# Message stage of a graph network kernel: units of four tiles and one of a single tile in place of four and three

## The chip, the cores and the metric

The kernel runs on one core of a Trainium2 chip. The time is that of one execution in microseconds of device time (us); a lower one is better. Its engines are PE (TensorE, matrix products), DVE (VectorE), ACT (ScalarE), POOL (GpSimd) and SP (SyncE, which here only issues DMAs). Each works through its own instructions in order and waits for others by semaphores.

## The reference

Two graph layers on 6250 nodes with 128 features, over 200000 edges sorted by destination:

```
h = relu(layernorm(x));  x = x + gcn2(relu(gcn1(h)))          # layer 0
h = relu(layernorm(x))                                         # layer 1
msg = relu(concat(h[src], edge_attr) @ W1 + b1)                # edge_attr: 32 columns
agg = segment_sum(msg, dst) / max(count, 1)
x = x + relu(concat(h, agg) @ W2 + b2)
```

The change touches only the third line and the sum in the fourth, the message stage. `h @ W1[:128] + b1` is made once per node, so a message is `relu(that[src] + edge_attr @ W1[128:])`.

## The kernel before, in words

The message stage treats the edges in two ways at once. The first half of the edges is sorted, earlier in the kernel, into 24 ranges; inside a range they lie in 49 tiles (blocks) of 128, each with edges whose sources fall in one block of 128 nodes. The other half is gathered: chunks of 512 edges, whose source rows POOL fetches by four indirect DMAs a chunk (`gather_messages`, line 779).

A loop runs over twelve pairs of ranges; eleven are one loop body, and the last is written out for itself. `UNIT_TILES = [4, 3] * 7` (line 84) cuts a range's 49 tiles into 14 units, so a pair has 28 units and 30 steps. In step u each engine has, in this order:

- PE: for an even chunk, the attribute products of two later chunks (`products_of`, line 1159); the transpose of unit u's attributes (`turn_attr`, 1183); a chunk's sums (`sums_of`, 1168); `block_products` of unit u-1, which is one product of the attributes with the weights, up to 512 columns (1190), and one product a tile of a one-hot matrix of sources with the node rows (1194); `block_sums` of unit u-2, one product a tile of a one-hot matrix of targets with the messages (1206).
- ACT: `message` of a chunk (1458), `stage_attr` of unit u+1 (1464), `take_attr` of unit u (1471), `block_message` of unit u-1 (1478), and at some steps the lows: `store_lows` (1300, 1302) and `load_lows` (1453).
- DVE: `source` of unit u, the one-hot matrix of sources (2187); `rest_of` unit u-2 (2177); a chunk's one-hot matrix; `target` of unit u-1 (2192); `add` (2157) and `products_in` (2200) of a chunk.

Pairs have 16 chunks, the last 24; `chunk_of(u, chunks)` spreads them evenly over the steps.

The "lows" are the numbers 0 to 127 of each edge's source in its block. They are turned by PE (`turn_lows`, at steps 7 and DU + 10), written to memory by ACT one step later, and read back spread over all partitions in four parts of `LO_UNITS = 4` units each. Parts 0 and 1 of the second range are loaded at step DU - 4, part 2 at DU - 2, part 3 at DU; those of the next pair's first range at steps 2 DU - 1, 2 DU and 2 DU + 1, the last three of a pair. `load_lows` first waits on ACT until the store has landed, and for parts 2 and 3 until part 0 or 1 of the same range has landed (they share a semaphore). `source` of a part's first unit waits for the part.

SP reads the next pair's two blocks of sorted edges (`load_blocks`, 617), each 833 KB, and the chunks' attributes (621), when semaphores of DVE and ACT let it.

Of the kernel before, what the change touches and what calls it, by code (L numbers as in the profile page):

```python
# [25 lines left out]
TC = 4  # L26
CE = TC * P
SLOTS = 8
# [34 lines left out]
SB = (N + P - 1) // P  # L63

RANGES = 24
RT = 32
DT = RANGES * RT
# [13 lines left out]
LATE_STEPS = (1, 2, 6, 8)  # L81
VISIT_ROWS_AT = 8
OWN_EDGE = 8192.0
UNIT_TILES = [4, 3] * 7
DU = len(UNIT_TILES)
LO_UNITS = 4
LO_PARTS = -(-DU // LO_UNITS)
LO_BLOCKS = sum(UNIT_TILES[:LO_UNITS])
LO_TURNED_AT = (7, DU + 10)
# [6 lines left out]
LAST_CHUNKS = (TURNS - FIRST_TURN) * SLOTS - (PAIRS - 1) * PAIR_CHUNKS  # L96
# [35 lines left out]
assert NP >= SB * P - 1 + P and TARGETS < SB * P and EP >= E and NCH % SLOTS == 0 and NT % (2 * HT) == 0  # L132
assert STRIPS % 2 == 1 and LAST_WIDTH % W == 0 and len(VISITS) == NW and KEYS <= 512 and SB == 12 * SEGS + 1 and STRIP % P == 0
assert SEG % BANKS == 0
assert DT % (SLOTS * TC) == 0 and LAST_CHUNKS % SLOTS == 0 and RANGES % 2 == 0 and DU % 2 == 0 and sum(UNIT_TILES) == SB and RT % 2 == 0
assert DT * P >= RANGE_ROWS
assert RANGES % 2 == 0 and LO_BLOCKS * P * 2 <= RT * ROW_WORDS * 4
assert all((b - a) * RT <= 512 for a, b in BLOCK_GROUPS) and RT * P < OWN_EDGE and RANKS_BEFORE_STARTS % RANK_BATCH == 0
# [4 lines left out]
def build(nc, t, out):  # L143
    with ExitStack() as ctx:
# [67 lines left out]
        def carve(columns, dt=F32):  # L212
            a = used[0]
            used[0] += columns
            assert used[0] <= SB * STRIP
            return region_a[:, a:a + columns].bitcast(dt)
# [21 lines left out]
        block_lo = [carve((SB + 1) // 2, BF16) for _ in range(2)]  # L238
        unit_attr = [carve(max(UNIT_TILES) * DE) for _ in range(2)]
        message_rows = carve(NT - DT, I32)  # L240
# [261 lines left out]
        def unit_tiles(u):  # L502

            first = sum(UNIT_TILES[:u])
            return first, UNIT_TILES[u]

# [1816 lines left out]
```

How the kernel before makes its waits and increments, by code:

```python
        def tables_stored(engine, n):  # L489
            for q in range(2):
                engine.wait_ge(tab_stored[q], 16 * ((NG + 1 - q) // 2) * (n + 1))
# [21 lines left out]
        def mixed_of(engine):  # L514
            engine.wait_ge(edges_read, 1)
            return engine.value_load(mixed_i[0:1, 0:1], min_val=0, max_val=1)
# [27 lines left out]
        def widen(engine, k, p):  # L545
            a, b = pieces_of(k)[p]
            at = k * len(PIECES) + p
            second = len(half_pieces(k))
            if p in (0, 1) and k:
                engine.wait_ge(C["loaded_a"], k * 16)
            if p in (second, second + 1) and k:
                engine.wait_ge(C["loaded_b"], k * 16)
            if at >= WIDE_SLOTS:
                engine.wait_ge(consumed, at - WIDE_SLOTS + 1)
            if len(APPLIED[k]) == 2:
                to, of = wide[:, at % WIDE_SLOTS, 0:b - a], count_pair[:, :, a:b].rearrange("p s h d -> p h s d")
            else:
                to, of = wide[:, at % WIDE_SLOTS].rearrange("p h s d -> p (h s) d")[:, 0:b - a], counts[0][:, a:b]
            if WIDENED_BY[p] == "act":
                nc.scalar.activation(to, of, ACT.Copy).then_inc(widened["act"], 1)
            else:
                nc.vector.tensor_copy(to, of).then_inc(widened["dve"], 1)
# [1 line left out]
        @block.sync  # L565
# [16 lines left out]
            load_bias("L0_gnn_b1")  # L582
            sp.wait_ge(rows_reduced, 1)
            sp.dma_start(tiles_dram[0].rearrange("(p q) -> p q", p=CR), row_min[0:CR, :]).then_inc(tiles_moved, 16)
```

## Time and profile before

| | us |
|---|---|
| three runs: median (lowest, highest) | 2529.35 (2528.84, 2536.39) |
| the profiled execution: its time | 2535.55 |
| its span, first to last instruction | 2533.6 |
| PE busy | 2189.9 (86%) |
| PE weight loads busy | 1792.7 (71%) |
| DVE busy | 1891.2 (75%) |
| POOL busy | 1840.9 (73%) |
| ACT busy | 1213.8 (48%) |
| mean granted clock of PE, full speed being 1 | 0.938 |

The busy times are of the profiled execution and overlap. "PE" are the matrix products, "PEld" the loads of their stationary operand. The granted clock has two levels, 2.4 and 1.2 GHz.

### The profile page before, as it was taken

The page shows a single profiled execution, that of the slowest core. Times are in us where ns is not written, and L with a number is a line of the kernel's source. Part 1 is how long each engine was busy: PE and PEld are TensorE (multiplying, and loading weights), DVE is VectorE, ACT ScalarE, POOL GpSimd, SP SyncE. Part 2 cuts the span into 40 slices and gives each one's busy share as a digit, 9 for nine tenths or more (in the row PEclk, how much of TensorE's full clock was granted, in tenths as well). Part 3 has the DMA queues.
Part 4 walks back from the last instruction along what each step waited for, and adds up shares of the span by engine and source line. Part 5 has one row for each costly group of instructions (what it writes and reads, how often), then busy time and mean ns, then how long its engine had stood idle before and what let it go on. Part 6 is the DMA issues. An engine that isn't in the chain of part 4 may idle for free.

```text
span 2533.6 us, 47549 instructions
## 1 busy us (share of the span) xinstructions
PE 2189.9 (86%) x15568; PEld 1792.7 (71%) x15569; DVE 1891.2 (75%) x3625; ACT 1213.8 (48%) x3289; POOL 1840.9 (73%) x1687
## 2 busy tenths in 40 slices
PE   0453799999999998699996699999999999999996
PEld 0132578997666898588885578778777877787785
DVE  6996999999888884644447577777777777777776
ACT  5842345665555775555553244444443444343340
POOL 0857777888888887777777577777777777777770
PEclk9665899999999999999997799999999999999998
DMA  9413223443332442488874243434343343434332
GB/s 366 155 42 128 72 73 123 156 149 123 121 119 109 145 173 74 133 311 307 318 275 158 85 142 103 124 118 127 117 121 118 96 126 116 138 98 122 116 90 61
DMA packets 127166, 357.85 MB, mean 141 GB/s; under 512 B 34082, under 2 KB 77831, under 8 KB 117687
## 3 DMA queue, kind: packets, MB, share of 16 engines
q10 hardware_dynamic: 24752, 186.56, 19.4%
q0 software_dynamic: 56880, 85.25, 13.0%
q1 hardware_dynamic: 45369, 84.00, 9.5%
q8 instruction: 83, 1.36, 0.2%
q14 instruction: 82, 0.67, 0.1%
HBM read 229.75 MB, written 125.93 MB: 140 GB/s over the span
## 4 chain that ended last, share of the span: by engine, by line
PE 67%; DVE 15%; DMA 6%; ACT 5%; issue 4%; POOL 2%; ACTq 0%; DVEq 0%; POOLq 0%; SPq 0%
PE ps_feat L1063 7%; PE ps_node L1063 6%; PE ps_sum L1168 6%; PE ps_node L1078 5%; PE ps_extra L1206 5%; DVE region_c L2002 4%; PE ps_feat L1078 4%; PE ps_node L1190 3%; PE pre_banks L1051 3%; PE ps_node L1194 3%; DMA rows_or_lows<-block_lows 3%; ACT rows L1282 3%; PE ps_feat L1190 3%; PE ps_sum L1194 3%; PE ps_sum L1190 3%
## 5 line engine op out<-in xcount | busy, mean ns | idle before, releaser
L797 POOL DMA_INDIRECT permuted<-rows_or_lows,slot_of_edge x768 | 923.4, 1202 | 234.1 <-issue 156.1
L779 POOL DMA_INDIRECT rows<-table,region_a x800 | 788.6, 986 | 291.1 <-issue 218.7
L2002 DVE TENSOR_TENSOR region_c<-iota_key,region_c 128x1568 bf16<-128x1568 f16 (+1 forms) x327 | 355.3, 1087 | 0.0
L1375 ACT ACTIVATE region_a<-pre_banks 128x392 bf16<-128x392 f32 x392 | 195.4, 501 | 198.8 <-PE pre_banks L1051 191.2
L1063 PE MATMUL ps_node<-region_a,region_b 128*128 128x256 bf16 (+1 forms) x1911 | 263.6, 268 | 0.0
L1063 PE MATMUL ps_feat<-region_a,region_b 128*128 128x256 bf16 x1764 | 254.4, 274 | 0.0
L563 DVE CAST wide_counts<-region_a 128x1024 fp32r<-128x1024 bf16 (+2 forms) x163 | 117.3, 724 | 156.7 <-PE ps_node L1078 65.7
L1206 PE MATMUL ps_extra<-msg_parts,target_hot 128*128 128x256 f32 x1176 | 222.4, 305 | 1.3 <-DVE msg_parts L2177 1.3
L561 ACT ACTIVATE wide_counts<-region_a 128x1024 fp32r<-128x1024 bf16 x150 | 158.4, 1060 | 121.3 <-PE ps_node L1078 52.7
L1168 PE MATMUL ps_sum<-onehot,rows 128*128 128x64 f32 x1600 | 209.2, 275 | 0.3 <-issue 0.2
L1168 PEld LDWEIGHTS ps_sum<-onehot,rows 128*128 128x128 f32 x1600 | 204.5, 199 | 5.5 <-issue 4.6
L2192 DVE TENSOR_TENSOR target_hot<-consts,region_a 128x512 fp32r<-128x512 f32 x336 | 207.3, 617 | 1.0
L1063 PEld LDWEIGHTS ps_node<-region_a,region_b 128*128 128x128 bf16 x1911 | 176.2, 97 | 28.7 <-issue 1.5
L1063 PEld LDWEIGHTS ps_feat<-region_a,region_b 128*128 128x128 bf16 x1764 | 169.5, 97 | 28.9 <-issue 0.4
L1478 ACT ACTIVATE msg_parts<-ps_node 128x512 fp32r<-128x512 f32 x120 | 65.4, 545 | 212.2 <-PE ps_node L1194 212.2
L1206 PEld LDWEIGHTS ps_extra<-msg_parts,target_hot 128*128 128x128 f32 x1176 | 161.6, 191 | 2.2 <-DVE msg_parts L2177 1.5
L1458 ACT ACTIVATE rows<-rows 128x512 f32<-128x512 f32 x200 | 124.9, 625 | 76.1 <-DMA rows_or_lows<-block_lows 31.9
L2200 DVE TENSOR_TENSOR rows<-rows,pre_banks 128x512 f32<-128x512 f32 x200 | 136.1, 680 | 18.1 <-DMA rows<-table,region_a 18.0
L2187 DVE TENSOR_SCALAR iota_units<-rows_or_lows,consts 128x512 f32<-128x512 bf16 x168 | 83.9, 499 | 86.8 <-PE ps_node L1194 55.7
L1078 PE MATMUL ps_node<-wide_counts,table_halves 128*128 128x512 f32 (+1 forms) x686 | 146.4, 374 | 1.6 <-DVE wide_counts L563 1.6
L1078 PEld LDWEIGHTS ps_node<-wide_counts,table_halves 128*128 128x128 f32 x686 | 122.1, 188 | 24.9 <-issue 1.8
L1478 ACT ACTIVATE msg_parts<-ps_sum 128x512 fp32r<-128x512 f32 (+1 forms) x108 | 59.5, 551 | 165.7 <-PE ps_sum L1194 165.7
(307 smaller groups left out, 4792.4 us busy)
## 6 DMA issues: line engine op xcount, KB each, us to landing
counts<-region_a ACTq DMA_DIRECT2D x23, 3136.0 KB
region_a<-counts ACTq DMA_DIRECT2D x11, 3200.0 KB, 12.1
region_a<-counts ACTq DMA_DIRECT2D x11, 3072.0 KB
rows_or_lows<-block_lows ACTq DMA_DIRECT2D x72, 448.0 KB
permuted<-region_b SPq DMA_DIRECT2D x25, 833.0 KB
region_a<-permuted SPq DMA_DIRECT2D x24, 833.0 KB, 4.9
rows_or_lows<-edge_cols_in POOLq DMA_DIRECT2D x24, 544.0 KB
region_a<-attr_t_in SPq DMA_DIRECT2D x50, 256.0 KB
```

Of the source, the lines that this page charges most:

```text
L561: nc.scalar.activation(to, of, ACT.Copy).then_inc(widened["act"], 1)
L779: nc.gpsimd.indirect_dma_start(rows[:, s, j * D:(j + 1) * D], None, tables[2], bass.IndirectOffsetOnAxis(ap=message_rows[:, c * TC + j:c * ...
L797: nc.gpsimd.indirect_dma_start(permuted, bass.IndirectOffsetOnAxis(ap=slot_of_edge[:, r * RT + k:r * RT + k + 1], axis=0), edge_rows_of[:, ...
L1063: ins = mm(strip_bank(buf)[:, 0:width], parts[:, h, k], counts[buf][:, h, 0:width], start=(h == 0 and k == 0), stop=(h == SB - 1 and k == ...
L1078: ins = mm((ps_feat if k % 2 else ps_node)[:, 0:width], halves[:, h, j], blocks[:, h - a], start=(h == 0 and j == 0), stop=(h == SB - 1 an ...
L1168: last = mm(ps_sum[0][:, 0:CW], rows[:, c % SLOTS, j * D:(j + 1) * D], onehot[:, c % 2, j, 0:CW], start=(j == 0), stop=(j == TC - 1))
L1190: mm(banks[u % 3][:, 0:n * D], attr_turned[u % 2][0:n * DE, :], edge_w[0:n * DE, 0:n].rearrange("p j d -> p (j d)"), start=True, stop=Fals ...
L1194: last = mm(banks[u % 3][:, j * D:(j + 1) * D], source_hot[u % 2][:, j * P:(j + 1) * P], messages_of[:, b0 + j], start=False, stop=(j == n ...
L1206: last = mm(ps_extra[:, 0:2 * D], target_hot[:, u % 2, j], msg_parts[:, u % 2, j].rearrange("p h d -> p (h d)"), start=(u % DU == 0 and j ...
L1375: nc.scalar.activation(counts[strip % 2][:, :, j * W:j * W + W], count_banks[w % BANKS][:, 0:KEYS].rearrange("p (d h) -> p h d", h=SB), AC ...
L2002: v.tensor_tensor(hot_key(u)[:, :, 0:n], iota_key[:, None, 0:n].to_broadcast([P, UNIT // SIDE, n, SIDE]), keys[:, :, None, :].to_broadcast ...
L2192: v.tensor_tensor(target_hot[:, u % 2, 0:n], iota[:, None, :].to_broadcast([P, n, P]), block_dst[u // DU][:, b0:b0 + n].unsqueeze(2).to_br ...
```

## The change

The units of a range become twelve of four tiles and one of a single tile. All that is written in terms of `DU`, `PAIR_UNITS` and `PAIR_STEPS` follows: `DU` is 13, a pair has 26 units and 28 steps. A part of the lows is then 16, 16, 16 and 1 blocks instead of 14, 14, 14 and 7. The other constants stand: the store of the next pair's lows comes at step DU + 11, which was step 25 of 0 to 29 and is step 24 of 0 to 27; parts 0 and 1 are loaded at 2 DU - 1, which was step 27 and is step 25. With sixteen chunks on 28 steps, chunks 14 and 15 still fall in the last two steps.

```
-UNIT_TILES = [4, 3] * 7
+UNIT_TILES = [4] * 12 + [1]
 DU = len(UNIT_TILES)
 LO_UNITS = 4
...
-assert ... and RANGES % 2 == 0 and DU % 2 == 0 and sum(UNIT_TILES) == SB and RT % 2 == 0
+assert ... and RANGES % 2 == 0 and sum(UNIT_TILES) == SB and RT % 2 == 0
```

## Rows read from the trace of the kernel before

**Rows 1.** The page, busy time of each engine (share of the span) and instructions.

```profile
PE 2189.9 (86%) x15568; PEld 1792.7 (71%) x15569; DVE 1891.2 (75%) x3625; ACT 1213.8 (48%) x3289; POOL 1840.9 (73%) x1687
```

**Rows 2.** Stretches: bounds, length, busy time and instructions, PE clock, DMA share, GB/s.

```profile
1512.00:2389.00 877.00, 849.95 (x5767) 692.66 (x5766) 650.41 (x1430) 355.94 (x1026) 647.73 (x658) 0.98 0.40 119
```

**Rows 3.** Chain of waits, 1700 to 1900: start, length, engine, tile, line, count.

```profile
1783.32 0.91 PE ps_sum L1190 x2
1784.23 0.89 PE ps_sum L1194 x8
1785.59 0.65 PE ps_node L1190 x2
...
1789.53 0.91 PE ps_feat L1190 x2
...
1791.81 0.65 PE ps_sum L1190 x2
...
1794.54 0.91 PE ps_node L1190 x2
...
1849.53 0.70 PE ps_feat L1190 x2
...
1851.48 0.86 PE ps_sum L1190 x2
```

**Rows 4.** Order of time at a pair's end: start, length, engine, line, operation, idle before.

```profile
1762.50 0.60 ACT L1478 ACTIVATE msg_parts<-ps_node 128x512 fp32r<-128x512 f32 x1 [1.48 <-PE ps_node L1194]
...
1763.28 0.29 ACTq L1302 DMA_DIRECT2D block_lows<-per_node  x1
...
1766.26 0.33 SPq L617 DMA_DIRECT2D region_a<-permuted  x1
...
1767.23 0.60 PE L1206 MATMUL ps_extra<-msg_parts,target_hot 128*128 128x256 f32 x3
1767.51 0.60 ACT L1478 ACTIVATE msg_parts<-ps_sum 128x512 fp32r<-128x512 f32 x1 [1.48 <-PE ps_sum L1194]
1767.72 0.82 ACTq L1453 DMA_DIRECT2D rows_or_lows<-block_lows  x2
...
1768.14 0.69 DVE L2177 SCALAR_TENSOR_TENSOR msg_parts<-ps_sum,msg_parts 128x512 fp32r<-128x512 f32 x1 [1.28 <-ACT msg_parts L1478]
...
1774.55 0.33 ACTq L1453 DMA_DIRECT2D rows_or_lows<-block_lows  x1
...
1777.00 0.31 PE L1183 MATMUL ps_feat<-consts,region_a 128*96 128x128 f32 x1 [2.15 <-ACT region_a L1464]
```

**Rows 5.** Waits, 1500 to 2400: who waited for whom: total us, times, longest.

```profile
ACT rows L1458 <- DMA rows_or_lows<-block_lows: 31.9, 11, 3.5
...
PE ps_feat L1183 <- ACT region_a L1464: 22.1, 11, 3.6
```

**Rows 6.** Waits of the last pair, 2390 to 2484.

```profile
DVE rows L2200 <- DMA rows<-table,region_a: 3.6, 1, 3.6
```

**Rows 7.** DMA issues of the whole span: count, KB each, median us to landing.

```profile
region_a<-permuted SPq DMA_DIRECT2D x24, 833.0 KB, 4.9
...
table<-rows SPq DMA_DIRECT2D x26, 256.0 KB, 2.3
```

**Rows 8.** Packets, MB, DMA share: SP's queue q1, 1768.1 to 1770.1; then both, 1770.1 to 1772.7.

```profile
q1 hardware_dynamic: 103, 0.63, 80.7%
...
q10 hardware_dynamic: 160, 0.54, 59.5%
...
q1 hardware_dynamic: 18, 0.07, 6.9%
```

**Rows 9.** Chain of waits behind the next pair's end.

```profile
1865.27 1.71 PE ps_node L1194 x8
```

**Rows 10.** Stretches of 10 us about the resumption, three of the eleven; clock third from last.

```profile
1602.00:1612.00 10.00, 7.51 (x51) 5.79 (x51) 6.28 (x15) 3.97 (x12) 7.56 (x9) 1.00 0.51 169
...
1859.00:1869.00 10.00, 7.37 (x39) 5.55 (x38) 5.20 (x11) 2.89 (x9) 7.72 (x8) 0.83 0.51 168
...
2383.00:2393.00 10.00, 7.89 (x36) 6.18 (x37) 4.30 (x12) 2.65 (x8) 7.81 (x8) 0.70 0.51 160
```

More of the change, by code:

```diff
@@ L134 @@
 assert SEG % BANKS == 0
-assert DT % (SLOTS * TC) == 0 and LAST_CHUNKS % SLOTS == 0 and RANGES % 2 == 0 and DU % 2 == 0 and sum(UNIT_TILES) == SB and RT % 2 == 0
+assert DT % (SLOTS * TC) == 0 and LAST_CHUNKS % SLOTS == 0 and RANGES % 2 == 0 and sum(UNIT_TILES) == SB and RT % 2 == 0
 assert DT * P >= RANGE_ROWS
```

## The prediction

> **What bounds the kernel now.** I read the page first, then the message stage by stretches, the chain of waits, the order of time around the end of a pair, and the waits in total.
>
> TensorE is busy 86% of the whole span, but the change touches only the message stage, 1426 to 2478 us. There the 877 us stretch that holds all eleven changes from one pair to the next has PE busy for 850 us [rows 1, 2]. So PE sets the pace, and what counts is its work and where it stands still. Inside a pair it never stands: the starts of the attribute products of consecutive units lie 2.27 us apart (a four-tile unit's products, then three-tile sums) or 1.95 us (three, then four) when the step has no chunk, 2.73 with a chunk's sums, 3.94 with the chunk's products and sums [rows 3].
>
> It stands at the end of each pair. ACT issues parts 0 and 1 of the next range's block numbers ("lows") right behind the message of unit 26, which starts at 1767.51; I call that moment T. Part 2 may go only when part 0 has landed, so ACT, an in-order engine, is stuck until 1774.55, and PE starves for the attributes that ACT stages behind it until R = 1777.00, which is T + 9.5 [rows 4]. All eleven ends show it: ACT waits 31.9 us in all for that DMA, and PE stands 22.1 us in all before the transpose, 2.0 each [rows 5].
>
> **The change, part by part.** Its own time is made against the profiled execution (2535.55 us, span 2533.6), and the same difference is then put on the median, 2529.35, 6.2 lower; the three runs lie 7.5 us apart, so the difference is worth more than the level.
>
> (a) Two units a pair fewer. Matrix work is per tile and stays: 49 tiles a range. What goes is a unit's own share. From rows 3: the attribute product takes 0.86 us with four tiles and 0.65 with three, 0.21 a tile, and the one-hot products of line 1194 take 0.89 for four, 0.22 a tile, so p = 0.436 a tile. 2.27 = 4p + 3s + o and 1.95 = 3p + 4s + o give s = 0.116 a tile for the sums and o = 0.18 a unit (the transpose and the exposed weight loads). Bounds on o: 0.1 to 0.3. Two units x 0.18 = 0.36 us a pair. Over eleven pairs -4.0 us. The twelfth gives nothing: in it VectorE stands 3.6 us for a gather, the last one [rows 6], so POOL sets its end. Fewer instructions on ACT and DVE are off the path.
>
> (b) The cover at the end of a pair shrinks. Steps counted from the end are the same before and after: last unit staged in step end-3, parts 0 and 1 issued in end-2, part 2 in end-1, part 3 in the last; chunks 13, 14 and 15 also keep their places. But what PE does between T and R is less: the last unit's products have one tile, not three (-0.87), its sums too (-0.23), and one sums group ahead of them has four tiles, not three (+0.12): -0.98 us. The length T to R is set by the DMA and not by PE, so this 0.98 us of work moves outside it. Per pair: +0.98 - 0.36 = +0.62 us, x 11 = +6.8 us. So taking work off PE gives time back only outside the stretch, and the two tiles that leave the last unit are paid in full.
>
> (c) Does T to R keep its 9.5 us? Three things act on when part 0 lands. Part 0 has 16 blocks instead of 14, 512 KB instead of 448. The 833 KB block read, issued 1.25 us ahead of T [rows 4], now lies one tile's products less its wider target earlier, about 0.3 us. The store of the lows is issued one step before the load and not two: it comes 0.78 us behind a message start, the load 0.21 behind the next [rows 4], and a step without a chunk lasts about 2.39 (2.27 + s), so the load would come 1.8 us behind the store instead of 4.4. The nearest row for how long a small write takes is 2.3 us for 256 KB [rows 7]: a wait between 0 and 0.5 us, I take 0.2. The extra 64 KB: by the two landings of rows 7 (577 KB more take 2.6 us longer) 0.29 us as an upper end, 0.1 as a lower. Sum 0.2 + 0.15 - 0.3 = about 0, with ends -0.3 and +0.8, so -3 to +9 us over eleven.
>
> The trace says that part 0 waits for the block read: issued at 1767.72, it has no packet from 1768.1 to 1770.1, in which SP's queue moves 103, and from 1770.1 to 1772.7 the picture is reversed, 160 packets of its queue against 18 [rows 8]. The Trainium skill, "DMA: Bandwidth & Descriptors", section "Queues, rings and completion order", has each DMA engine go round robin between queue rows packet by packet. By that rule parts 0 and 1 would share at once, the block read's start would not matter, and the sum of this part would be +0.35 us an end, 3.8 us more in all; the trace does not agree in these two microseconds, so I keep the head start.
>
> (d) The granted clock. After a long stand PE runs at half speed for a while: eight of the same matmuls take 1.71 us behind one pair's end and 0.89 behind another's [rows 3, 9]. In the 10 us around R the granted clock is 1.00 at four ends, 0.83 at two and 0.66 to 0.71 at five, one of each in [rows 10]. 0.83 means 3.4 us at 1.2 GHz, 0.70 some 6 us; at most half of it is lost, 1.7 and 3.0, and a little less where PE still waits in it: I take 1.5 and 2.8 us, so 17 us are lost this way now. The end of rows 4, with a stand of 2.15 us, keeps the full clock, and the mean stand is 2.0; with 0.98 us more the mean is 3.0, on the side of the longest of now, 3.6 [rows 5]. I let two of the four fall to the long form (+5.6) and one short one become long (+1.3): +7 us. Ends: 0 (nothing falls) and +14 (all eleven long, 31 - 17).
>
> (e) Around the one-tile unit inside a pair (units 11 to 13). Sums of unit 11 need ACT's and DVE's pass over its products: the message starts 0.28 us behind the products' end (the sums start at 1767.23, the message at 1767.51), the rest is done at 1768.14 + 0.69, so 1.6 us in all [rows 4]. PE has in between the sums of unit 10 (0.47), a transpose (0.11), a chunk's sums (0.78; chunk 7 falls in that step) and one tile's products (0.5): 1.86 us. It just fits: 0, and 0.5 us each if it does not. Lows of the second range are issued at step 9 and asked for two four-tile steps later, about 5.6 us against 5 now, where no wait shows: 0. POOL gathers sixteen chunks a pair and is not made faster or slower; longer stands only give it more slack.
>
> (f) Start and tail: the first pair waits for the table and gathers as before: 0. The last unit's tail has two tiles less, under 0.5 us.
>
> Sum: -4.0 + 10.8 + 0 + 7 = +13.8 us. 2529.35 + 13.8 = 2543 us.
>
> **The rivals.** *The one-tile unit starves PE in mid-pair.* For it: the cover of (e) is only 0.25 us over the need. Against: the chunk's sums fall there, and no chain wait shows inside a pair now [rows 3]. 0.5 us at 12 mid-pair places and again behind them, some 12 us: 2555.
>
> *Everything at the end goes badly.* The store is late (+0.8 an end) and all ends drop the clock: 6.8 + 9 + 14 = +30: 2559.
>
> *Not slower: landing follows the block read.* If part 0 lands a fixed time behind the block read and not behind its own issue (the two windows of rows 8 speak for it), the read's head start counts in full, the store's wait vanishes in it, and T to R shortens by 0.3 or more. It decides from the point where the read is drained later than the load's issue plus its own start time, which is so in rows 8. Then 6.8 - 3.5 = +3.3, stands are barely longer and the clock stays: 2533. Against it: the 64 KB come on top.
>
> *Units were dearer than I think.* If o is 0.3 and more, and T to R shortens by 0.6 with the clock falling less often, the sum is -6.6 + 10.8 - 6.6 - 5 = -7: 2522. Only the unlucky phase of the clock at five ends speaks for it.
>
> **How the numbers follow.** A difference of 0.3%, 7.6 us, is about what a measurement here can tell from none. My forecast 0.52 (its own range 2537 to 2551), the starving unit 0.14, all bad at the end 0.10, landing behind the block read 0.17, dear units 0.07. Slower by over 0.3%: 0.52 less its lower edge (0.04) + 0.14 + 0.10 + 0.02 (the upper part of the block-read case) = 0.74. Same: 0.04 + 0.15 = 0.19. Faster 0.07. The range 2531 to 2559 leaves out the fastest rival and part of the bad end.
>
> **What would show it.** Right: 26 transposes and attribute products a pair; starts 2.4 us apart in steps without a chunk, about 3.2 with a chunk's sums and 4.4 with both; the stand before the transpose at the pair's end near 3 us and 11 times; T to R about 9.5 us; more of the eleven windows under 1.00. Wrong: (b) if T to R shrinks with PE's work; (c) if the load waits for the store by more than 0.8 us, or part 0 lands over 0.5 us sooner or later behind its issue; (e) if block sums of units 11 or 12 wait for DVE; the whole, if the eleven pair ends lie closer together than now.

## The result and the profile after

The changed kernel takes 2563.56 us (median of four runs, 2562.20 to 2564.21); the kernel before, four runs beside them, 2531.18 (2528.84 to 2536.39). The ratio is 1.0124, 95% interval 1.0107 to 1.0142: slower, by 32 us where 13.8 were forecast, and above the range. The two profiled executions differ by 26.7 us in span, 2560.3 against 2533.6; before's lay 4 us above its median and after's 1 below, which makes up the rest.

The page of the changed kernel, answering to [rows 1]. PE is busy 13 us longer, with the same products a tile and 72 instructions fewer:

```profile
PE 2202.9 (86%) x15496; PEld 1784.5 (70%) x15497; DVE 1886.6 (74%) x3553; ACT 1200.1 (47%) x3217; POOL 1873.4 (73%) x1687
```

Its message stage by stretch, answering to [rows 2], the same 877 us. The clock (third from last) is 0.96 and was 0.98, and fewer of PE's instructions come through, 5579 against 5767 (some 60 of the 188 are the two units a pair that are gone, six instructions a pair):

```profile
1512.00:2389.00 877.00, 848.58 (x5579) 675.62 (x5580) 631.81 (x1340) 337.23 (x946) 653.99 (x643) 0.96 0.39 115
```

The chain of waits inside a pair, answering to [rows 3] (start, length, engine, tile, line, count). From one attribute product to the next it is 2.39 us without a chunk, 4.39 with a chunk's products and sums, 3.23 with its sums. Those are the forecast's 2.4, 4.4 and 3.2:

```profile
1794.72 0.91 PE ps_sum L1190 x2
...
1797.11 0.86 PE ps_node L1190 x2
...
1801.50 0.91 PE ps_feat L1190 x2
...
1804.73 0.91 PE ps_sum L1190 x2
```

So the inside of a pair came out as forecast. The end of a pair, in order of time, answering to [rows 4]:

```profile
1774.25 0.33 SPq L617 DMA_DIRECT2D region_a<-permuted  x1
...
1774.69 0.29 ACTq L1302 DMA_DIRECT2D block_lows<-per_node  x1
...
1776.24 0.60 ACT L1478 ACTIVATE msg_parts<-ps_node 128x512 fp32r<-128x512 f32 x1 [0.68 <-PE ps_node L1194]
...
1779.40 0.82 ACTq L1453 DMA_DIRECT2D rows_or_lows<-block_lows  x2
1780.33 0.63 ACT L1458 ACTIVATE rows<-rows 128x512 f32<-128x512 f32 x1 [3.49 <-DVE rows L2200]
...
1781.20 1.08 PE L1168 MATMUL ps_sum<-onehot,rows 128*128 128x64 f32 x8 [1.11 <-ACT rows L1458]
...
1783.37 1.96 PE L1159 MATMUL pre_banks<-edge_w,region_a 64*128 64x256 f32 x8 [0.81 <-DVE rows L2200]
...
1783.87 0.33 ACTq L1453 DMA_DIRECT2D rows_or_lows<-block_lows  x1
...
1786.34 0.48 PE L1183 MATMUL ps_feat<-consts,region_a 128*128 128x128 f32 x1 [1.01 <-ACT region_a L1464]
```

Parts 0 and 1 of the lows are issued 3.16 us behind T (1776.24), where it was 0.21. The message of the chunk names DVE as its releaser, but its rows had been done: ACT's own queue is in order, and what stood ahead was the wait for the store to land, issued at 1774.69, 0.44 us behind the 833 KB block read. The store of 12 KB and its load lie 4.7 us apart. In return part 2 may go 4.47 us after the load's issue, not 6.8, since the block read is over by then. T to R is 10.1 us here and 10.12 in the mean of the eleven ends, against 9.34 before, where the first end alone has 10.92; without the first it is 10.13 against 9.18. The read itself is not slower: by its packets it runs 4.1 to 6.8 us from its issue at the eleven ends, and ran 4.2 to 6.4 before.

Where PE stood moved with it. The waits from 1500 to 2415 (who for whom: total us, times, longest), answering to [rows 5]: the stand of 2 us before the transpose has become two of about 1 us, on a chunk's sums and before the transpose, and the short one on a chunk's products has grown; 31.5 us in all, where it was 22.1 and 4.9, 27.0 us.

```profile
ACT rows L1458 <- DVE rows L2200: 37.0, 11, 3.9
...
ACT rows L1458 <- DMA rows_or_lows<-block_lows: 27.4, 9, 3.3
...
PE ps_sum L1168 <- ACT rows L1458: 13.4, 11, 1.9
...
PE ps_feat L1183 <- ACT region_a L1464: 9.7, 11, 2.0
...
PE pre_banks L1159 <- DVE rows L2200: 8.4, 11, 0.8
```

The short one in the kernel before, from 1500 to 2400:

```profile
PE pre_banks L1159 <- DVE rows L2200: 4.9, 11, 0.5
```

The 10 us from 4 us ahead of R, three of the eleven, answering to [rows 10]. Every one of the eleven ends is at a lowered clock, where four kept it before; low time at the eleven ends adds up to 81.9 us (41.0 before):

```profile
1604.30:1614.30 10.00, 7.16 (x35) 5.07 (x35) 5.05 (x11) 2.95 (x9) 7.76 (x8) 0.83 0.53 180
...
1870.80:1880.80 10.00, 8.42 (x35) 5.73 (x35) 4.56 (x11) 2.81 (x9) 7.56 (x9) 0.66 0.52 186
2227.00:2237.00 10.00, 8.28 (x31) 6.09 (x30) 4.10 (x10) 2.22 (x7) 7.56 (x9) 0.51 0.58 182
```

Behind such an end the chain of waits has an attribute product of 1.81 us where 0.86 to 0.91 is usual, the same kind of row as [rows 9]:

```profile
1788.57 1.81 PE ps_node L1190 x2
```

And one line that the forecast took as unchanged, the gathers of POOL (count | busy, mean ns of one | idle), 1020 ns each; they took 986 before:

```profile
L779 POOL DMA_INDIRECT rows<-table,region_a x800 | 815.8, 1020 | 283.8 <-issue 229.5 <-PE pre_banks L1159 23.2 <-DVE rows L2200 12.4
```

In the last pair DVE then waits more for them, answering to the 3.6 us of [rows 6]:

```profile
DVE rows L2200 <- DMA rows<-table,region_a: 8.3, 4, 4.1
```

**Where the 26.7 us of the two spans lie.** R and T read off at each end give the sum: to the first R +0.3. From R to T at full clock 76.25 us before, and 77.0 after (78.68 at the end with only 3.4 us of lowered clock, half of it taken off): +0.75, ten times 7.5. T to R +0.95 in the ends 2 to 11, ten times 9.5. What R to T takes beyond its full-clock value in the mean, 1.42 us before (77.67) and 2.13 after (79.13), is the clock behind R: +0.7, ten times 7.1. From the last R to the end, 146.8 before and 149.1 after: +2.3.

### The profile page after: what moved, and what is told of

Read it like the earlier page. It is cut to its first block, busy times and chain, and to the rows that moved or that the text cites. A ratio compares the mean times of both kernels' runs of the same rounds, so it can differ in the third digit from the quotient of the medians.

```text
span 2560.3 us, 47121 instructions
## 1 busy us (share of the span) xinstructions
PE 2202.9 (86%) x15496; PEld 1784.5 (70%) x15497; DVE 1886.6 (74%) x3553; ACT 1200.1 (47%) x3217; POOL 1873.4 (73%) x1687
## 3 DMA queue, kind: packets, MB, share of 16 engines
q0 software_dynamic: 56880, 85.25, 12.7%
## 4 chain that ended last, share of the span: by engine, by line
PE 67%; DVE 15%; DMA 6%; ACT 5%; issue 4%; POOL 2%; ACTq 1%; DVEq 0%; POOLq 0%; SPq 0%
PE ps_feat L1063 6%; PE ps_sum L1168 6%; PE ps_node L1063 6%; PE ps_node L1078 6%; PE ps_feat L1078 5%; PE ps_extra L1206 5%; DVE region_c L2002 4%; PE pre_banks L1051 4%; PE ps_node L1190 3%; PE ps_node L1194 3%; ACT rows L1282 3%; PE ps_feat L1190 3%; PE ps_sum L1190 3%; PE ps_sum L1194 3%; PE ps_feat L1194 3%
## 5 line engine op out<-in xcount | busy, mean ns | idle before, releaser
L779 POOL DMA_INDIRECT rows<-table,region_a x800 | 815.8, 1020 | 283.8 <-issue 229.5
L1168 PE MATMUL ps_sum<-onehot,rows 128*128 128x64 f32 x1600 | 214.7, 280 | 13.8 <-ACT rows L1458 13.4
L1206 PE MATMUL ps_extra<-msg_parts,target_hot 128*128 128x256 f32 x1176 | 216.9, 304 | 3.5 <-DVE msg_parts L2177 3.4
L2192 DVE TENSOR_TENSOR target_hot<-consts,region_a 128x512 fp32r<-128x512 f32 (+1 forms) x312 | 203.9, 653 | 1.0
L1478 ACT ACTIVATE msg_parts<-ps_node 128x512 fp32r<-128x512 f32 (+1 forms) x108 | 60.7, 562 | 189.3 <-PE ps_node L1194 189.3
L1159 PE MATMUL pre_banks<-edge_w,region_a 64*128 64x256 f32 x800 | 123.8, 432 | 24.2 <-DVE rows L2200 23.3
L1478 ACT ACTIVATE msg_parts<-ps_feat 128x512 fp32r<-128x512 f32 (+1 forms) x108 | 60.5, 560 | 163.4 <-PE ps_feat L1194 163.4
```

Source lines behind the costliest of these rows:

```text
L779: nc.gpsimd.indirect_dma_start(rows[:, s, j * D:(j + 1) * D], None, tables[2], bass.IndirectOffsetOnAxis(ap=message_rows[:, c * TC + j:c * ...
L1168: last = mm(ps_sum[0][:, 0:CW], rows[:, c % SLOTS, j * D:(j + 1) * D], onehot[:, c % 2, j, 0:CW], start=(j == 0), stop=(j == TC - 1))
L1206: last = mm(ps_extra[:, 0:2 * D], target_hot[:, u % 2, j], msg_parts[:, u % 2, j].rearrange("p h d -> p (h d)"), start=(u % DU == 0 and j ...
L2192: v.tensor_tensor(target_hot[:, u % 2, 0:n], iota[:, None, :].to_broadcast([P, n, P]), block_dst[u // DU][:, b0:b0 + n].unsqueeze(2).to_br ...
```

## The experiments

The theory when they began: three costs, namely the cover taken from the end of the pair, the store that lands late because it is issued behind the block read, and the clock that falls with both. T is the start of the last four-tile message, R the transpose at which PE resumes. Short names: "before" and "after" are the two kernels. Ratios are to the kernel before on the same chip. The experiments ran on several chips, and the kernel before had medians from 2531.2 to 2538.5 us beside them, so the gap between two experiments is also given by their ratios, 1% being 25.3 us; the intervals of the ratios are 0.1 to 0.4% to either side.

**1. The store a step earlier, in the changed kernel.**

```
-LO_TURNED_AT = (7, DU + 10)
+LO_TURNED_AT = (7, DU + 9)
```

> The changed kernel with the next pair's lows turned and stored one step earlier (LO_TURNED_AT's second entry DU + 9 instead of DU + 10), so that the store is again two steps ahead of the load, as before the change. Theory Q (the store is queued behind the 833 KB block read, and parts 0 and 1 wait for it): store to load about 4.7 us stays by construction, but the load is issued 0.2 us behind T and not 3.2; T to R goes from 10.2 back to about 9.3 us, eleven times 0.9 = 10 us, and with the clock lowered a little less: about 2550 us. Rival S (parts of 512 KB or the cover alone lengthen the end, the store does not matter): T to R stays 10.2 and the time 2563 us.

Measured 2555.70 us (six runs, 2549.65 to 2560.88), ratio 1.0087 (1.0065 to 1.0109). T to R is back at 9.3 us in the ends 2 to 11 (11.5 at the first), and the store's wait is gone: parts 0 and 1 go 0.21 us behind T. Its net cost is 8 us of the 32 by the medians and 9 by the ratios. PE's stand is one again, 23.6 us in eleven; with 12.7 us on the chunk's products it is 3.3 us an end, where the kernel before has 2.5: +0.85, near the 0.98 of (b).

**2. The store a step later, in the kernel before.** The two steps between store and load become one.

```
-LO_TURNED_AT = (7, DU + 10)
+LO_TURNED_AT = (7, DU + 11)
```

> The kernel before with that store one step later (DU + 11), all else as it was: the store's part of the change alone. Q: the store is issued behind the block read and lands more than 4 us later, parts 0 and 1 go out about 3 us behind T, T to R grows from 9.3 to about 10.2 us, the clock falls at more ends: 2541 to 2548 us. S: 2531 us, no difference.

Missed with its sign: 2517.93 us (2510.19 to 2520.77), ratio 0.9935 (0.9912 to 0.9957). In this order of time at a pair's end the store goes 0.09 us *ahead* of the block read, and the loads follow 2.35 us later, nearly on time:

```profile
1757.55 0.31 ACTq L1302 DMA_DIRECT2D block_lows<-per_node  x1
1757.64 0.33 SPq L617 DMA_DIRECT2D region_a<-permuted  x1
1759.21 0.60 ACT L1478 ACTIVATE msg_parts<-ps_sum 128x512 fp32r<-128x512 f32 x1 [0.76 <-PE ps_sum L1194]
...
1759.90 0.82 ACTq L1453 DMA_DIRECT2D rows_or_lows<-block_lows  x2
```

At nine ends of the eleven it is 2.1 to 2.7 us, but at two 3.8 and 5.3. The number of steps is therefore not the cost; what decides is where a 12 KB store lies against an 833 KB read, within half a microsecond, and at this place it is still late now and then. PE stands 12.5 us before the transpose where it stood 22.1, T to R is 8.6, and low time 20 us for 41. Why it gains 16 us is open: part 0 lands 5.3 us behind its issue in the mean, where it took 6.6, and the transposes of the lows (`turn_lows`) come a step later, which puts more of PE's work beside the transfers; no run takes the two apart.

**3. The one-tile unit last, in the kernel before, all else as it was.** 28 units; the parts of the lows follow the units and have 14, 14, 16 and 5 blocks.

```
-UNIT_TILES = [4, 3] * 7
+UNIT_TILES = [4, 3] * 4 + [4] * 5 + [1]
```

> The kernel before, still 14 units a range and the store where it was, but units of 4,3 four times, then five of 4 and one of a single tile last (the parts' bounds follow the units): the cover's part of the change alone. Theory C (TensorE's work between T and R is what shrinks; T to R is fixed by DMA): +0.98 us of work outside per pair, 11 us, and about 7 us by the clock: 2548 us, T to R about 9.3 us. Rival: the store alone makes the loss, then 2531 us.

Measured 2548.18 us (nine runs, 2540.78 to 2553.62), ratio 1.0048 (1.0028 to 1.0067). The number is the expected one, but the kernel before lay higher on this chip (2533.59): two tiles fewer at the end of a range cost 12 us by the ratio and 15 by the medians, not 17. The parts did not come as expected either: R to T at full clock is 77.56 us, +1.3 for the 0.98 expected; T to R is 7.9 to 9.0, 8.55 in the mean and 0.8 shorter; and low time is 44 us, hardly above the 41 of before.

**4. The one-tile unit first, in the changed kernel.**

```
-UNIT_TILES = [4] * 12 + [1]
+UNIT_TILES = [1] + [4] * 12
```

> The changed kernel with the single-tile unit first instead of last, 13 units, store still late. C: three tiles' products and sums more lie under the stretch T to R, 1.7 us a pair off the rest, 19 us in all, and a lower clock at fewer ends: about 2538 us. Rival (the loss is the store's alone): 2563 us less nothing.

2549.33 us (2540.96 to 2553.31), ratio 1.0059 (1.0036 to 1.0082): between the two expectations. 14 us come back with the cover (16 by the ratios); the store stays 0.44 us behind the read, T to R is 9.4 to 12.0, and that part stays.

**5 and 6. The block read held until part 0 of the lows is loaded**, in the kernel before and in the changed one. SP waits for part 0 of the next pair's first range before it issues the second read, which puts the read 6 to 7 us later.

```
+                        sp.wait_ge(B["lo_loaded_0"], k * 64 + 80)
                         load_blocks(k + 1, 1)
```

> The kernel before, with the block read of the next pair's second range held back on SP until part 0 of the lows has landed. Theory Q, as it stands after the first four runs (parts 0 and 1, and with a late store the store too, queue behind the 833 KB block read; TensorE resumes some 10.5 us behind the read's issue whatever else moves): part 0 lands about 3 us behind its issue, no ACT wait at part 2, no stand before the transpose, no lowered clock at the pair's end: 27 us of stands and about 18 us by the clock gone, about 2488 us. Rival (part 0 needs its 6.7 us by itself): 2531 us.

> The same edit in the changed kernel. Q: the stands go, the store lands in about 2 us, and what is left of the change is two units' own share a pair, 0.36 us, so 0 to 4 us below the same edit in the kernel before, about 2485 us. Rival M (the one-tile unit or the larger parts cost in themselves): 5 us or more above it.

In the kernel before 2511.88 us (2508.37 to 2513.34), ratio 0.9916 (0.9890 to 0.9942). Nine of the ten periods from R to R take 83.4 us (85.0 to 89.0 before), PE no longer stands before the transpose, and no clock is lowered before 2380 us: the collision of the read with the lows was the whole of that stand. It misses the expected 2488 by 24 us, and 15 of them lie behind the last R, from which it is 161.8 us to the end, where it was 146.8. The waits of the last pair, 2345 to 2454, name POOL's gathers:

```profile
DVE rows L2201 <- DMA rows<-table,region_a: 21.2, 12, 3.8
...
PE ps_extra L1207 <- DVE msg_parts L2178: 9.3, 4, 2.6
```

In the changed kernel 2530.71 us (2526.20 to 2536.95), ratio 0.9992 (0.9975 to 1.0008), 19 above its fellow where 0 to 4 below was expected: a miss, and rival M is right. A period is 85.4 us for 83.6, with R to T at full clock 77.0 for 76.1, which is the cover, and a stand of 0.6 us left before the transpose. But what sets the end in both kernels is POOL. From the first gather to the last it takes 1057 us here and 1039 there, and 800 times (1017 ns and the 0.30 us between two gathers) is already 1054, with 994 ns it is 1035. So 18 of the 19 us are the longer gathers, and from here on they are a floor under the whole stage.

**7. One tile first and the store a step earlier, in the changed kernel** (the edits of 4 and 1).

> The changed kernel with both costs of the pair's end undone: the single-tile unit first, and the store one step earlier. Both parts: the last unit has four tiles, one more than before the change, so more work lies under the stretch; T to R 9.3 us, two units' share saved: -0.36 - 0.58 us a pair against before, 10 us, and a lower clock at fewer ends: about 2520 us. If the parts did not add (something else of thirteen units costs): 2535 us or more.

2532.25 us (2528.17 to 2537.68), ratio 0.9999 (0.9980 to 1.0018). With cover and store mended, the change costs nothing and brings nothing. The gain is there and is given back: a period is 85.6 us for 86.85, 12 us in ten, but from the last R to the end it is 157.7 us for 146.8, because POOL, with gathers of 1018 ns here too, takes 1058 us from its first gather to its last, as in 6.

**8 and 9. The stand filled with idle products**, in the kernel before and in the changed one: 24 small bf16 products that write unused columns, in the stretch in which PE waits.

```
+                        if u == 1:
+                            for _ in range(24):
+                                mm(ps_turn[:, 256:256 + P], zero_bf[:], ident_bf[:], start=True, stop=True)
```

> The kernel before with 24 small bf16 products (zeros times a unit matrix, into unused columns, nobody waits for them) in front of the transpose at which TensorE stands at a pair's end, about 1.3 us of work inside a stand of 1.4 to 3.6 us. Theory K (the lowered clock behind the stand is worth about 18 us in eleven ends): hardly any end drops, 10 to 15 us faster, about 2518 us. Rival (the clock behind the stand costs little): 2531 us or a little more.

> The changed kernel with the 24 small products of run e8 in front of the transpose at the pair's end. The changed kernel has a lowered clock at all eleven ends, 82 us in all against 41 before. Theory K: the drops grow shorter or go, some 20 us off 2563, 2540 to 2550 us; since the stands are longer than the filling and lie in two more places, some drops stay. Rival (what the change lost lies in stands and not in the clock): under 5 us off.

In the kernel before 2517.87 us (2515.49 to 2520.14), ratio 0.9938 (0.9916 to 0.9959), as expected, with no lowered clock at the eleven ends, where there were 41 us. R to T is 76.23 us in the mean where it was 77.67: 14 us in ten periods, near the 17 of eleven ends worked out from [rows 10]. The stretch, answering to [rows 2]:

```profile
1512.00:2389.00 877.00, 866.82 (x6147) 709.04 (x6148) 663.69 (x1460) 363.17 (x1046) 657.21 (x669) 1.00 0.41 120
```

In the changed kernel 2562.18 us (2558.65 to 2566.85), ratio 1.0119 (1.0079 to 1.0158): no gain, a miss. The filling sits before the transpose; the two stands ahead of it are left, and low time is still 64.9 us:

```profile
PE ps_sum L1168 <- ACT rows L1461: 17.6, 11, 3.1
...
PE pre_banks L1159 <- DVE rows L2203: 7.2, 11, 0.8
```

Yet behind R it did what it should: R to T is 77.0 us in the mean where it was 79.1, at its full-clock value, so the clock behind R costs the changed kernel 21 us in ten periods and the kernel before 14. The filling gave this back ahead of R. It met the lowered clock at nine ends of the eleven, took up to 2.74 us there and not the 1.51 of experiment 8, and held up the transpose: T to R is 12.1 us in the ends 2 to 11 for 10.1. The same 24 products, at an end of 8 and at one of 9:

```profile
1770.48 1.51 PE L1225 MATMUL ps_turn<-ident_bf,zero_bf 128*128 128x128 bf16 x24
```

```profile
1788.19 2.43 PE L1225 MATMUL ps_turn<-ident_bf,zero_bf 128*128 128x128 bf16 x24
```

**10. The store behind the block read, in the kernel before.**

```
-LO_TURNED_AT = (7, DU + 10)
+LO_TURNED_AT = (7, DU + 12)
```

> The kernel before with the store two steps later (DU + 12), so that it is issued more than a microsecond behind the 833 KB block read, in the step of the load itself; units as before. Run e2 (one step later) put it 0.1 us ahead of the read, where it landed in 2.2 us. Theory Q: now it waits behind the read, lands 4 us or more after its issue, parts 0 and 1 go out 4 to 5 us behind T and TensorE resumes 12 us or more behind the read's issue, against 10.6: 2 us an end and a clock lowered at every end, 2565 us or more. Rival (the store's landing is short wherever it lies): the load goes out 2.3 us behind the store, about 2540 us.

2548.42 us (2538.11 to 2564.84), ratio 1.0057 (1.0029 to 1.0084); it brings the late load of the changed kernel into the kernel before, 3.3 to 6.2 us behind T, and a T to R of 11.0 us in the mean (10.1 to 13.0). The time expected, 2565 or more, was too long, though PE does resume 12.5 us behind the read's issue. The store is late to a varying degree: its load follows it by 2.5 to 3.1 us at seven ends and by 4.3 to 5.4 at four. The same view as in 2, at one of the seven:

```profile
1771.84 0.33 SPq L617 DMA_DIRECT2D region_a<-permuted  x1
1773.39 0.60 ACT L1478 ACTIVATE msg_parts<-ps_sum 128x512 fp32r<-128x512 f32 x1 [1.48 <-PE ps_sum L1194]
...
1774.18 0.29 ACTq L1302 DMA_DIRECT2D block_lows<-per_node  x1
1776.88 0.82 ACTq L1453 DMA_DIRECT2D rows_or_lows<-block_lows  x2
```

**11. Late store and filling together, in the kernel before** (the edits of 2 and 8).

> The kernel before with the two edits that gained by themselves: the store one step later (e2, 2518 us) and the filling products (e8, 2518 us). Both work through the same stand and the same clock: if K holds they don't add, since with either most of the clock's loss is gone: 2510 to 2516 us. If they were independent: about 2502 us.

2513.12 us (2508.07 to 2518.90), ratio 0.9924 (0.9892 to 0.9956), as expected, and no lowered clock at the eleven ends.

**12. Part 0 with sixteen blocks, in the kernel before.**

```
-UNIT_TILES = [4, 3] * 7
+UNIT_TILES = [4] * 4 + [3] * 4 + [4, 3] * 3
```

> The kernel before with its fourteen units in another order: four of four tiles, four of three, then four and three by turns three times. The parts of a pair's load are then 16, 12, 14 and 7 blocks; unit count, the last two units (four, three) and the store's step are those of before. Part 0 is 512 KB a range in place of 448, as in the changed kernel. Theory (part 0's bytes lengthen the stretch from the last four-tile message to the next pair's first transpose): about 0.5 us more at each of eleven ends, and perhaps one or two more drops of the clock at 2.8 us: 2538 to 2542 us. Rival (the bytes cost nothing, the 0.4 to 0.6 us more from part 0's issue to part 2's that two other kernels showed is scatter): 2531 us. Gathers: both expect about 986 ns, as in all kernels of fourteen units.

2534.74 us (twelve runs, 2527.23 to 2536.98), ratio 0.9999 (0.9986 to 1.0011). The rival is right: 64 KB more in part 0 cost nothing that shows, and T to R is 7.7 to 9.7, 8.9 in the mean. The 0.15 us of the forecast was, if anything, too much, and the +0.95 us in the changed kernel goes to the store; experiment 1, with the same part 0 and the store early, has 9.3.

**13 to 15. DVE's four-tile target operation in two halves**, on top of 6 (the changed kernel with the read held), alone in the changed kernel, and on top of 5.

```
-v.tensor_tensor(target_hot[:, u % 2, 0:n], ..., ALU.is_equal).then_inc(B["target"], 1)
+for a, z in ((0, 2), (2, 4)) if n == 4 else ((0, n),):
+    last = v.tensor_tensor(target_hot[:, u % 2, a:z], ..., ALU.is_equal)
+last.then_inc(B["target"], 1)
```

> The changed kernel with the block read of the next pair held until the lows of the pair are loaded (2530.71 us), and DVE's target operation of a four-tile unit issued as two operations of two tiles. Theory (a long DVE operation keeps GpSimd's gathers back, which is why they take 1017 to 1031 ns in kernels of thirteen units and 979 to 994 ns in those of fourteen): the gathers' mean falls to about 990 ns, and the last pair, which GpSimd sets, is shorter; time 2515 to 2522 us, the split's own cost on DVE included. Rival (the gathers' length has nothing to do with the length of DVE's operations): gathers stay near 1017 ns, time 2531 us or some us more by the added DVE instructions.

> The changed kernel (2563.56 us) with DVE's target operation of a four-tile unit issued as two operations of two tiles, and nothing else. Theory (the long operation is what stretches the gathers from 986 to 1020 ns): the mean of the gathers falls to about 995 ns and the stretch from the last pair's first transpose to the end, 149.1 us, to 146 or less; the eleven ends keep their late store, so the time falls by 3 to 8 us, to 2556 to 2560. Rival (the gathers set nothing here while the ends stall): the mean falls but the time stays within 2 us of 2563.6.

> The kernel before with the block read of the next pair held until the lows of the pair are loaded (2511.88 us), and the target operation of its four-tile units in two. Theory: the gathers' mean falls below the 994 ns of that kernel and its last pair, which GpSimd sets, ends earlier: 2502 to 2508 us. Rival (with half of the units of three tiles the long operation is seldom in the way, and the split only adds instructions to DVE): 2512 us or a little more.

13 gave 2520.42 us (2518.81 to 2526.04), ratio 0.9945 (0.9927 to 0.9963), 10 us under 6 (12 by the ratios) with 288 DVE instructions more. First the gathers of 6, then of 13, both in the page's columns:

```profile
L780 POOL DMA_INDIRECT rows<-table,region_a x800 | 813.4, 1017 | 259.2 <-issue 232.0 <-DMA table<-region_c 15.6 <-DVE agg L2158 6.1
```

```profile
L780 POOL DMA_INDIRECT rows<-table,region_a x800 | 795.4, 994 | 262.4 <-issue 223.9 <-DVE rows L2203 14.9 <-DMA table<-region_c 13.1
```

The operation itself, first in 6 and then in 13: one of 682 ns became two of 418.

```profile
L2193 DVE TENSOR_TENSOR target_hot<-consts,region_a 128x512 fp32r<-128x512 f32 x288 | 196.6, 682 | 1.0
```

```profile
L2194 DVE TENSOR_TENSOR target_hot<-consts,region_a 128x256 fp32r<-128x256 f32 x576 | 216.8, 418 | 1.0
```

14 gave 2560.04 us (2557.11 to 2562.13), ratio 1.0089 (1.0066 to 1.0113), 3.5 us under the changed kernel by the medians and 9 by the ratios, about the expected 3 to 8. The gathers took 989 ns, 24.5 us less in all, and the stretch from the last R to the end 144.8 us, 4.3 less, while the ends stayed as they were. So the 27 us by which the gathers are longer than before are not by themselves the 32 that the change costs. 15 gave 2500.22 us (2496.74 to 2503.74), ratio 0.9851 (0.9828 to 0.9875): below its expected 2502 to 2508 and 38 us under the kernel before on this chip, the fastest kernel of the study. Its gathers take 976 ns, and from the last R to the end it is 148.5 us where 5 took 161.8.

## Why the prediction was wrong

The direction was right, and so was the place, the end of a pair; the size was too small by 13 us in the two spans and 19 in the medians. The failed step is (c): T to R was put at no change and grew by 0.95 us an end, 9.5 of the 13 us. The tail gives 2.3 more; the 6 us between spans and medians are where the two profiled executions lay among their runs.

- **(a) and (b), units and cover: right.** Inside a pair the starts came as worked out. Outside T to R a pair is 0.75 us longer, forecast 0.62. Experiment 3, the cover alone, gave 12 to 15 us, but with T to R 0.8 us shorter, which the forecast had named as a sign against (b); the read lies 0.42 us further ahead of T there, and in experiment 1, where it does so too, T to R is 9.3. What shortened it in 3 stays open.
- **(c) T to R: wrong, the main miss.** "The nearest row for how long a small write takes is 2.3 us for 256 KB [rows 7]: a wait between 0 and 0.5 us, I take 0.2." The row is of an earlier stage of the kernel, where no 833 KB read was issued just ahead; with that read held the 12 KB store does take 2.1 to 2.4 us (6). The prediction moved the store past a queue and priced it by its size and its distance in steps; but one step's shift also turned its order with the block read round. Before, it went 2.98 us ahead of the read (1763.28 and 1766.26 in [rows 4]); after, 0.44 behind. Its load then waited 3.16 us behind T where 0.21 was before, six times the upper bound. Experiment 2 has one step between store and load as well, and at nine ends of eleven the load goes within 1 us of T: the store was 0.09 us ahead. The price is not 3 us an end, since the loads land 2.3 us sooner once the read is over: +0.95, just above the outer end of +0.8. The read's head start did not save it: its issue lies 1.99 us ahead of T, not 1.55, and R still came later. The 64 KB were priced at 0.15 us and cost none that experiment 12 could tell. Of the round robin between queues that the forecast cites it says that "the trace does not agree in these two microseconds". About 1 us of them is a load's own start: with the read held, the first packet of part 0 goes 1.0 to 1.5 us behind its issue, and it went 2.4 to 2.9 behind in the kernel before.
- **(d) The clock: the number by luck.** +7 was forecast with two or three ends changed; all eleven drop, and what shows behind R is +7.1. Its upper case (all eleven long, +14) is nearer the picture. Experiment 8 supports the 17 us lost before: 14 in ten periods. The length of the stand, by which (d) chose its ends, does not order the drops: before, the end with 2.15 us kept the full clock and one with 1.40 lost it.
- **(e) The one-tile unit inside a pair: right in its place.** No chain wait shows at units 11 to 13. **"POOL gathers sixteen chunks a pair and is not made faster or slower": wrong.** 1020 ns for 986, 2.3 us in the last pair (the forecast's (f) has 0), 3.5 to 9 by experiment 14, and 18 once the ends are healed (6 against 5).
- **Rivals.** The landing does follow the block read, as the not-slower rival had it, but this works against the store too; experiments 5 and 6 show that the read is the cause of the stands. "Everything at the end goes badly" was nearest in form, 2559; its +0.8 an end for the store is near the 0.95 measured.

Do the pieces add up? By the ratios the store alone gives back 9 us (1), the cover alone 16 (4), both together 32 (7), which is the whole loss. The sum is 6 us short of it, and the four intervals together leave 10 us on that difference, so it may be nothing (by the medians it is 9). If it is real, the clock is what both share: low time at the eleven ends is 82 us after, 75 in 1, 34 in 4 and 17 in 7. That is argued from these sums, not shown by a run.

## What to carry to other kernels

When an edit shifts a small DMA by a step, place it in the merged order of all queues, and not by its size: half a microsecond behind a large read, the small store here held its load 2 to 3 us longer than with no read ahead. Take work off a bottleneck engine only where it does not cover a transfer, and look for the transfer whose start collides with the one that is waited for; holding the block read for a few microseconds was worth more than any regrouping of the units. Before an operation of DVE is made longer, see what POOL does beside it, and when one engine's stands are healed, see which engine is the next floor: here 800 gathers with their gaps.

## What the runs showed of the hardware

**Small store, large read.** Answering to [rows 8]: in the changed kernel, 1773.4 to 1779.5, the traffic by queue (packets, MB, share of the 16 engines); q1 is SP's, q10 ACT's, whose 56 packets here are the store's and go out from 1777.1 to 1778.6, the first 2.4 us behind its issue:

```profile
q1 hardware_dynamic: 288, 1.12, 53.7%
...
q10 hardware_dynamic: 56, 0.01, 1.0%
```

Over the eleven ends the first packet goes 2.4 to 3.7 us behind the issue, and 0.9 to 1.2 with the read held (6). From store to load it took 2.1 to 2.4 us with the read held (6); 2.1 to 2.7 at nine ends and 3.8 and 5.3 at two with the store 0.09 us ahead of the read (2); 4.4 to 5.5 at 0.44 behind (the changed kernel); 2.5 to 3.1 at seven ends and 4.3 to 5.4 at four at 2.34 behind (10). The Trainium skill, "DMA: Bandwidth & Descriptors", section "Queues, rings and completion order", has each DMA engine go round robin between queue rows by packet, with typically 9 to 17 descriptors in a packet. If what the profile counts are such packets, the store would have had its turn early, and the trace does not agree. If they are descriptors, the read's 288 are 18 an engine, a turn or two are the whole read, and the trace agrees. No run here tells which.

**Gathers beside a long DVE operation.** In kernels of thirteen units with the whole operation the gathers take 1017 to 1021 ns (the changed kernel, 4, 6, 7, 9) and 1031 (1); with fourteen units 979 to 994, and 976 with the operation halved (15); with thirteen and the operation halved, 994 and 989 (13, 14). The Trainium skill, "SBUF — State Buffer", section "Who interferes with whom", says that a DVE instruction with two inputs in SBUF contends with a GpSimd instruction that reads SBUF, and calls the shared pair of ports an exclusive lock. The trace agrees as far as it goes: halving the instruction, which has two inputs in SBUF, takes 23 ns (13) and 31 ns (14) off a gather. No run changed the number of its inputs, so the port itself is not shown, and the same section tells of a probe in which an instruction of this kind did not stall a DMA.

**The granted clock behind several short stands.** Before, a stand of 2 us an end and one of up to 0.5 left the full clock at four ends of eleven; after, three of 0.8 to 1.2 us in the mean left it at none, 31.5 us of stands in place of 27. Idle products in the stand kept it at all eleven (8), and the time fell by some 16 us. Where the clock was down before they began (9), they took up to 2.74 us for 1.51 and gained nothing.
